# Selective scan on one NeuronCore: the decay exponents of two of four state groups are multiplied on TensorE

## What is computed

```python
def step(h, inp):                      # h: [sequence, channel, state]
    dt_t, B_t, C_t, u_t = inp
    dA = jnp.exp(jnp.clip(dt_t[:, :, None] * A, -20.0, 0.0))
    dB_u = jnp.clip(dt_t[:, :, None] * B_t[:, None, :] * u_t[:, :, None], -10.0, 10.0)
    h = jnp.clip(h * dA + dB_u, -100.0, 100.0)
    y = jnp.einsum('bdn,bn->bd', h, C_t)
    return (h, y)
```

## Time and profile before

| | us |
|---|---|
| median of three runs | 2129.08 |
| the profiled execution's own time | 2125.4 |
| its span in the trace | 2123.6 |
| of it, the scan of states (first decay to last keep_y) | 1346.6 to 1706.2 |

### The profile page before, as it was taken

One profiled execution on the slowest core, in us unless ns is written; L12 is line 12 of the kernel. 1 busy time (PEld: TensorE's weight loads), 2 busy tenths in 40 slices (PEclk: granted clock), 3 DMA queues, 4 the chain that ended last, 5 costly groups with the idle time before them and its releaser, 6 DMA issues. The chain is left out here.

```text
span 2123.6 us, 37416 instructions
## 1 busy us (share of the span) xinstructions
PE 1705.6 (80%) x11541; PEld 1100.6 (52%) x11568; DVE 1418.0 (67%) x3093; ACT 968.1 (46%) x2622; POOL 477.9 (23%) x497
## 2 busy tenths in 40 slices
PE   5999999999999399878889585577777734499998
PEld 3666666666666155445555474465565624244443
DVE  3666666666666366657677444799999975577776
ACT  2555555555555133323233235899999901011110
POOL 0111111111111010000000011688888843000000
PEclk9999999999999699989989798798989966699999
DMA  3101010010100550000056100000000000100000
GB/s 80 31 20 30 20 30 27 23 30 20 30 20 11 169 165 0 16 6 0 0 167 197 61 0 0 1 1 0 1 1 0 0 10 0 46 6 6 10 6 15
DMA packets 69410, 66.57 MB, mean 31 GB/s; under 512 B 5753, under 2 KB 66896, under 8 KB 69328
## 3 DMA queue, kind: packets, MB, share of 16 engines
q1 hardware_dynamic: 66516, 64.00, 9.9%
q10 hardware_dynamic: 2812, 1.66, 0.3%
HBM read 61.45 MB, written 4.19 MB: 31 GB/s over the span
## 5 line engine op out<-in xcount | busy, mean ns | idle before, releaser
L1836 PE MATMUL ss_y_ps<-ss_h,ss_diag 128*128 128x256 f32 x1024 | 265.2, 423 | 133.0 <-ACT sc_dt L1754 93.5
L418 ACT ACTIVATE x_probs<-x_s_ps,x_neg_max 128x257 f32<-128x257 f32 x512 | 238.4, 471 | 251.3 <-DVE x_neg_max L489 251.3
L1836 PEld LDWEIGHTS ss_y_ps<-ss_h,ss_diag 128*128 128x128 f32 x1024 | 216.4, 214 | 181.5 <-issue 90.7
L489 DVE TENSOR_REDUCE x_neg_max<-x_s_ps 128x2 f32<-128x514 f32 x256 | 174.3, 681 | 179.2 <-PE x_s_ps L288 179.2
L1738 ACT ACTIVATE ss_decay<-sc_dt,sc_a 128x256 f32 (+1 forms) x496 | 206.2, 466 | 1.8 <-DVE ss_h L1801 1.8
L496 DVE COPY x_pT<-x_pT_ps 128x512 f32<-128x512 f32 x256 | 175.5, 686 | 42.6 <-PE x_pT_ps L298 38.4
L285 PE MATMUL x_s_ps<-x_kT,x_qblk 32*128 32x257 f32 x1024 | 182.6, 433 | 0.0
L1792 DVE SCALAR_TENSOR_TENSOR ss_decay<-ss_decay,ss_h 128x1024 f32<-128x1024 f32 x124 | 152.4, 1229 | 29.3 <-ACT ss_decay L1738 29.1
L298 PE MATMUL x_pT_ps<-all_ident,x_probs 128*128 128x128 f32 x1024 | 169.9, 289 | 0.6 <-ACT x_probs L418 0.5
L1748 ACT ACTIVATE ss_come<-ss_dtu,sc_xd 128x256 f32<-128x256 f32 x384 | 162.7, 502 | 6.6 <-POOL ss_dtu L1694 6.6
L1708 POOL TENSOR_TENSOR ss_diag<-all_ident,sc_xd 128x512 f32<-128x512 f32 x128 | 160.7, 1256 | 11.4 <-PE ss_y_ps L1836 1.4
(11 more groups left out here) (357 smaller groups left out, 3223.3 us busy)
## 6 DMA issues: line engine op xcount, KB each, us to landing
x_ctx_t<-ctxT SPq DMA_DIRECT2D x48, 514.0 KB, 3.8
kept_ctx_t<-ctxT SPq DMA_DIRECT2D x16, 514.0 KB, 8.3
kept_ctx_n<-ctx SPq DMA_DIRECT2D x16, 512.0 KB, 8.7
x_ctx_n<-ctx SPq DMA_DIRECT2D x16, 512.0 KB, 3.9
all_x<-x SPq DMA_DIRECT2D x4, 512.0 KB, 7.1
x_mid<-all_x SPq DMA_DIRECT2D x32, 64.0 KB, 3.6
all_x<-x_mid SPq DMA_DIRECT2D x4, 512.0 KB, 7.5
out<-all_x SPq DMA_DIRECT2D x8, 256.0 KB, 2.1
```

The source lines that it names most:

```text
L418: ins = nc.scalar.activation(probs[p][:, n, :], s_ps[u % 2][:, j, 0:S2], ACT.Exp, bias=neg_max[p][:, n:n + 1], accum_out=sums[p][:, n:n + 1])
L489: vec.tensor_reduce(neg_max[p][:, 2 * u:2 * u + 2], s_ps[u % 2][:, :, 0:S2], AX.X, ALU.max, negate=True).then_inc(max_sb, 1)
L1836: ins = nc.tensor.matmul(y_ps[p][:, 0:DI], diag[q][:, m, :], h[q][:, m, :], start=(q == 0 and m == 0), stop=(q == NQ - 1 and m == NH - 1))
```

## The change

Groups 0 and 2 (WIDE) no longer get their products from the scale operand of the four exps. POOL builds once, before the positions, `rates`: for each of the eight rates the identity times the rate, a stationary operand of 128x128. For each position PE multiplies `rates` with `dt` into the slot of the ring (**power**, four fp32 matmuls of 256 columns), and ACT takes one exp of 1024 columns in place, PSUM to PSUM. Groups 1 and 3 are as before. The wait for the ring slot moves, for the two groups, from ACT to PE, and ACT waits for PE instead. PE's order becomes, for position t: power 0 of t, unit 0 and unit 1 of t-1, power 2 of t, unit 2 and unit 3 of t-1, and after the last position the four units of position 31. PE now loops over six positions like the others.

```diff
+WIDE = (0, 2)
...
+        rates = sb("rates", [P, len(WIDE), NH, P])
...
+            for w, q in enumerate(WIDE):
+                nc.gpsimd.tensor_tensor(rates[:, w, :, :], g.ident[:, :].unsqueeze(1).to_broadcast([P, NH, P]),
+                                        a[:, q * NH:(q + 1) * NH].unsqueeze(2).to_broadcast([P, NH, P]), ALU.mult).then_inc(rates_sb, 1)
...
             def decays(t, k, q):
                 n = (t - 1) * NQ + q
+                if q in WIDE:
+                    act.wait_ge(power_psum, (t - 1) * len(WIDE) + WIDE.index(q) + 1)
+                    d = decay[ring(k, q)]
+                    nc.scalar.activation(d[:, :], d[:, :], ACT.Exp).then_inc(decay_psum, 1)
+                    return
...
+            def power(t, k, q):
+
+                n = (t - 1) * NQ + q
+                if not (isinstance(n, int) and n < RING):
+                    pe.wait_ge(h_sb, n + NQ - RING + 1)
+                for m in range(NH):
+                    ins = nc.tensor.matmul(decay[ring(k, q)][:, m * DI:(m + 1) * DI], rates[:, WIDE.index(q), m, :], dt[:, t, :],
+                                           start=True, stop=True)
+                ins.then_inc(power_psum, 1)
...
-            for t in range(2):
+            def position(t, k, first=False, last=False):
                 for q in range(NQ):
-                    unit(t, t, q)
-            with pe.Fori(1, T // 2) as i:
-                for p in range(2):
-                    for q in range(NQ):
-                        unit(i * 2 + p, p, q)
+                    if q in WIDE:
+                        power(t, k, q)
+                    unit(t - 1, k - 1, q)
+
+            pe.wait_ge(rates_sb, len(WIDE))
+            positions(pe, position)
+            for q in range(NQ):
+                unit(T - 1, T - 1, q)
```

More of the change, by code:

```diff
@@ L1670, in scan_states @@
         decay_psum, kept_psum, h_sb = (sem(n) for n in ("decay_psum", "kept_psum", "h_sb"))
+        rates_sb, power_psum = sem("rates_sb"), sem("power_psum")
         y_psum, y_sb = sem("y_psum"), sem("y_sb")
@@ L1829, in _, with unit @@
         def _(pe):
-            def unit(t, p, q):
+            def power(t, k, q):
[6 more added lines that the diff above has]
+                ins.then_inc(power_psum, 1)
+            def unit(t, k, q):
                 pe.wait_ge(h_sb, t * NQ + q + 1)
@@ L1835, in unit @@
                 for m in range(NH):
-                    ins = nc.tensor.matmul(y_ps[p][:, 0:DI], diag[q][:, m, :], h[q][:, m, :],
+                    ins = nc.tensor.matmul(y_ps[k % 2][:, 0:DI], diag[q][:, m, :], h[q][:, m, :],
                                            start=(q == 0 and m == 0), stop=(q == NQ - 1 and m == NH - 1))
                 ins.then_inc(y_psum, 1)
-            for t in range(2):
+            def position(t, k, first=False, last=False):
                 for q in range(NQ):
-                    unit(t, t, q)
-            with pe.Fori(1, T // 2) as i:
-                for p in range(2):
-                    for q in range(NQ):
-                        unit(i * 2 + p, p, q)
+                    if q in WIDE:
[5 more added lines that the diff above has]
+                unit(T - 1, T - 1, q)
 def scan_output(nc, g, uz, y):
```

## The result

The changed kernel takes 2132.13 us (median of 20 runs), the kernel before 2128.53 in as many: a ratio of 1.002, with a 95% interval of 1.0013 to 1.0027. That is 3.6 us more. The interval lies above 1, so the changed kernel is slower, but by less than the 0.2% (4.3 us) that counts as no change. The forecast was 2131.1 us.

A forecast was written before the change was run, and what follows sets the result against it. The prediction took ACT to bound the kernel at 11.43 us a position, then a loop of 11.51. Loop +2.2, start -1.1 and end +0.9 made +2.0 us, 2131.1 us on the median; range 2124 to 2146.

The forecast's parts named there:

- The bound before, ACT at 11.43 a position: Scan of states before the change: ACT's seven sets of four and one keep_y set the pace, 11.43 us a position.
- The loop of kept 0, state 1, power 0, wide exp: Once a position over DVE, PE and ACT: sets the new pace, 11.51 us against 11.433, +2.2 us in all.
- kept 0 to the end of state 1: The loop's stretch on DVE: 8.33 us in the rows, 8.26 without a wait of 0.07 for decays 2.
- POOL's eight operations and dt_u are hidden as before: POOL's work in each position: adds no time, since ACT's raws come no later.
- The start, -1.1: First positions of the scan: kept 0 starts 0.7 us earlier, and the way to position 2 saves another 0.4.
- The end, +0.9: From kept 0 of position 31 to the last keep_y: 15.36 us instead of 14.50, +0.9.
- Power at full clock: PE in the changed scan: stays at full pace, busy over 90% with a granted clock near 1.00.
- PE's sum: PE's work in each position: 48 instructions at 0.218 us each take 10.47 us at full pace.
- The waits: Idle times in each position: DVE some 0.7 us before kept 3 and 0.3 before kept 0, ACT about 1 before exp 0.
- PE as the bound: Slower rival: at the old mean clock PE needs 12.1 us a position, +20 us, so 2149; chance 0.18.
- The long hops: Slower rival: the handovers between engines take their upper bounds, loop 11.79 us, so 2139; chance 0.17.
- The ring that does not bind: Faster rival: DVE's own pace is left, 10.45 us a position with PE at 10.47, -28 us, so 2101; chance 0.06.

The follow-up runs named there:

- e10: The changed kernel without POOL's diagonals after position 0 and with POOL's clip of group 0 cut to one element; ratio 0.9997 to the kernel before.
- e3: The changed kernel with only group 0 wide, group 2 back to four exps; 2170.21 us, ratio 1.0205 to the kernel before.
- e1: The changed kernel with one matmul of power 0 done twice in each position; ratio 1.0085 to the kernel before.
- e2: The changed kernel with one matmul of unit 3 done twice in each position; ratio 1.0047 to the kernel before.
- e4: The changed kernel with groups 1 and 2 wide instead of 0 and 2; ratio 1.0124 to the kernel before.
- e8: The changed kernel with only group 2 wide; 2116.44 us, ratio 0.9954 to the kernel before.
- e9: The changed kernel with only group 2 wide and mine moved on DVE behind state 0; ratio 0.9982 to the kernel before.
- e11: The changed kernel with state 3 moved on DVE right behind state 2, ahead of the next kept 0; ratio 1.0015 to the kernel before.
- e5: The changed kernel with groups 1 and 2 wide and keep_y moved on ACT to after raw 1; ratio 1.0121 to the kernel before.

## Why the prediction was right

**The bound before, ACT at 11.43 a position:** right. Its busy time fell and the position did not follow it.

**The loop of kept 0, state 1, power 0, wide exp:** it is there, and its half from state 1 over power 0 to exp 0 decided the sign. But it does not set the pace. Predicted 11.51, it closes in 11.48 (e10); the changed kernel runs at 11.63, by the loop that leaves it at exp 0 and returns over raw 0, POOL's clip and mine. Its terms: the way from state 1 to the first matmul 0.15 (0.14), power 1.99 (1.97), to ACT 0.04 (0.08), the wide exp 1.01 (1.03), to kept 0 0.03 (0.03). The term that was mis-sized is "kept 0 to the end of state 1", 8.26 against 8.41. It was taken from rows in which mine started 0.07 after the clip ended; that an engine off the path could move into it when ACT's timing shifts was not looked at. The sentence "POOL's eight operations and dt_u are hidden as before" is the step that failed: they are hidden for those that wait for POOL's results, not for DVE's product of two SBUF tensors. The stretch was 0.15 short and the other terms together 0.03 long, so the loop was 0.12 short: 0.12 * 29 = 3.5 us of the trace's sum. The forecast's sum was +2.0; with the loop at 11.63 it is +5.5, and with the start at nothing in place of -1.1 it is +6.6, against 5.8 measured: over the 29 positions a mean of 11.605 stood where the loop gives 11.63, which is 0.7 of the rest. Both errors made the forecast too low. That 2131.1 still lies 1.0 from the measured 2132.13 is partly luck: the medians differ by 3.6, the scans by 5.8.

**The start, -1.1:** measured 0.0. Kept 0 of position 1 was 0.7 earlier, as said. The other 0.4 and the 0.7 itself were lost inside position 1: raw 0 waited 0.45 for dt_u, kept 1 waited 1.25 for decays 1, and the two first units ran at the lower clock (6.66 us for 16 instructions), so that power 2 and its exp were late.

**The end, +0.9:** 0.8.

**Power at full clock:** right, 0.99 in place of 0.89. PE's sum was a little low, 10.47 against 10.96 in the rows (3.65 + 1.83 twice), since each change between power and unit costs about 0.1 or more; it stayed beside the path.

**The waits:** kept 0 waits 0.38 (0.3 forecast), kept 3 0.49 (0.7), ACT 1.43 ahead of exp 0 (about 1).

**The rivals.** PE as the bound did not happen in this kernel, but e3 shows that the lowered clock, which that rival needed, is real in a neighbour of it. The rival had PE both full and slowed; in e3 PE has less to do, and the lowered clock falls on power 0. The long hops did not show. The ring that does not bind did not happen; e1 and e2 tell it apart. That the result is slightly slow and not level is the loop over POOL's clip: without it (e10) the ratio is 0.9997.

## What to carry to other kernels

Before work is moved to an idle engine, draw every loop through semaphores and queues that closes once an iteration, add it up from rows, and compare it with the busiest engine; an exact sum over one loop is worth more than busy shares, but the second and third loop must be summed too (e4, e8, e9 and e11 each ran into another one, and e5 moved an instruction that was in none). The group to move is the one with the most work between the event that frees its buffer and the one that wants it: with group 2 alone the same edit gives 0.9954 (group 1 has three operations there too, and was not tried alone). A moved engine's timing also moves what it collides with, so look at what runs on POOL beside each DVE instruction with two SBUF inputs.

## What was not expected of the hardware

- Less work made PE slower where it counts: with 20 matmuls a position power 0 took up to 3.67 us at a clock of 0.89, with four useless ones added 1.99 at 1.00, and the kernel was 29 us faster.
- A DVE product of two SBUF tensors that meets a running POOL instruction ended 1.07 to 1.09 us after it wherever it took longer than its own 1.23 in the scans of the kernel before, the changed kernel, e5, e8, e9 and e11, whether it started 0.29 before the clip's end (1.37 long) or 0.03 after its start (2.09). It works the other way too: a clip or the diagonals that start beside a running mine end 0.9 after it and take 1.89 to 2.13 instead of 1.04, as the diagonals at 1396.69 in the kernel before, where mine kept its 1.23.
- The same wait of power 0 for state 1 cost 0.15 us inside the loop and 0.06 in the positions written out at the end (power starts at 1695.17 after state 1 ended at 1695.11), which makes those positions 11.54 instead of 11.63.
